# A cross-attention kernel: scores from two fp32r parts in 64-row tiles in place of three bf16 parts

## The chip, the cores and the metric

The kernel runs on one core of a Trainium2 chip. The metric is device time in microseconds of one execution, the median of several runs; lower is better.

## What is computed

Two cross-attention blocks follow each other on the same context, for four batch entries. The first has layer norms, 16 heads of 16 columns, and an MLP with GELU; the second has one head over 256 columns. Cut to what matters here:

```python
# first block: x is 4 x 256 x 256, context 4 x 512 x 256
q = (layer_norm(x) @ q_w + q_b)          # 16 heads of 16
k = (ctx @ k_w + k_b)
v = (ctx @ v_w + v_b)
scores = einsum('bhqd,bhkd->bhqk', q, k) * 16 ** -0.5
attn = softmax(where(mask, scores, lowest), axis=-1)
h = (attn @ v) @ cproj_w + cproj_b + x
h = h + gelu(layer_norm(h) @ fc_w + fc_b) @ proj_w + proj_b
# second block, one head: softmax(h wq (ctx wk).T / 16) (ctx wv) wo
return h + alpha * delta
```

## The kernel before

The five engines have a program each, written out by hand, and meet at semaphores. The unit of order is a slot. A batch entry has NG = 4 groups of GH = 4 heads, a group has SLOTS = 8 slots, so 32 slots a batch entry; slot s of a group is head s // 2. Each engine walks the slots in `iteration` (three levels by batch entry: the entry's attention, the projections of the next one, `pre`, and the rest of both blocks of the one before, `post`). Tables say in which slot a step stands: PRE_AT and EARLY_AT for `pre`, POST_AT and LATE_AT for `post`, PREP_AT for weights, TAIL_AT for the last entry.

**Precision by parts.** Products of projections and MLP are made of two fp32r parts of each operand (high, and the rest) and three matmuls (`product` L585, `products` L593; lines L589, L602, L606). The scores are made otherwise: queries and keys are split in three bf16 parts each, and the six products of TERMS_Q and TERMS_K are stacked along the contraction: `q_stack` and `k_stack` hold per head 6 x 16 rows of parts, one row for the mask (ones against `mask_row`), and 12 rows for the row maxima (three bf16 parts of each of four heads' maxima in `q_stack`, selectors in `k_stack`), 109 rows in all. So one bf16 matmul gives the whole score.

**A group's way.** `max_tile` (TensorE, L652) computes scores with the queries stationary and 512 keys moving, 97 rows; VectorE's `take_max` (L1442) takes the negated maximum over the keys, from one of three banks of `s1`. After the eight tiles of a group POOL's `split_max` (L1763 to L1769, four short operations) splits the maxima into three parts in `max_cols`. `max_rows` (TensorE, L659) transposes them in two matmuls, ScalarE's `rows` (L1100) copies them into `q_stack`. Then `exp_tile` (TensorE, L669) computes the scores again the other way round, keys stationary and 256 queries moving, two matmuls a slot, with the maximum already taken off; ScalarE's `exp` (L1109) writes `probs`, and `pv` (TensorE, L679) multiplies by `vals` with the denominator's column of ones, four heads in four column tiles of 17 columns. The maxima of group g+1 are made in the slots in which the exponent tiles of group g are made (MAX_TILES: two tiles in slots 0 and 1, one in slots 2 to 5; the split in slot 5, the transposes in slot 6). In a slot TensorE's order is: max tiles, `pre`, `post` or weight step, exp tile, in slots 1 and 3 the value product, in slot 6 the transposes of the maxima.

**Queries and keys.** For the queries (`pre`, U_Q) ScalarE writes the value `qf` (L1070) and its high part (L1072), then frees the bank; POOL takes the rest (L1785), ScalarE the middle part (L1087), POOL the low part (L1789). For each half of the keys VectorE writes `kf` (L1421), ScalarE the high part (L1092), POOL the rest (L1793), ScalarE the middle part (L1096), POOL the low part (L1797). In the prologue VectorE does POOL's operations for the first.

**Stack transfers.** SP moves the parts into the stacks by DMA, 16 partitions and four heads at a time: per group six transfers of queries (`stack_queries`, L518), six of keys (L529) and one of the mask row (L523), 13 in all, after the group's exponent tiles of the batch entry before are done. In the prologue ScalarE's queue (L1083) and POOL's (L1876) issue some of them. The selector rows are written once (L1320, L1322).

The file's other names on which a step rests: `ft[2]`, the third scratch of the GELU, lies over `qf`, so POOL's third square waits for `q_parts`.

## Time and profile before

| | us |
|---|---|
| median of 3 runs | 314.64 |
| lowest and highest | 312.69, 316.79 |
| span of the profiled execution | 310.4 |
| TensorE (PE) busy in it | 268.6 |
| VectorE (DVE) busy | 206.8 |
| ScalarE (ACT) busy | 187.8 |
| POOL busy | 118.3 |

The profile is of one execution of its own, and its span runs from the first to the last instruction; the page gives no other time for it. Busy time of PE is the union of its matmuls' records, which overlap: a matmul's start is recorded, its end is modelled. So how fast TensorE goes is read from the distance of starts, and a busy PE may still stand between two matmuls. An x4 in a row of the timeline merges four instructions of one line; plain fp32 matmuls leave two records each. The moving type of fp32r matmuls reads f32 (those of L589, L602 and L606 are fp32r). A wait is put down to whoever came last.

### The profile page before, as it was taken

To read this page: it belongs to the slowest core of one execution; us is meant where nothing else is said; L and a number is where in the kernel's file an instruction comes from. 1 tells how busy PE (TensorE), PEld (TensorE's weight loads), DVE (VectorE), ACT (ScalarE), POOL (GpSimd) and SP (SyncE) were. 2 spreads that over 40 slices of the span, in tenths; PEclk is the share of its full clock that TensorE was granted. 3 is DMA by queue.
4 is the path that set the end of the run, shared out by engine and by line. 5 is a ranking of instruction groups with operands and counts; after the bars stand their busy time and mean duration, and the time that the engine had idled before them with its cause. 6 is when DMAs were issued, how large, how long until landed. Compare 5 with 4: busy or idle time off the path is not lost.

```text
span 310.4 us, 5591 instructions
## 1 busy us (share of the span) xinstructions
PE 268.6 (87%) x2073; PEld 195.3 (63%) x2073; DVE 206.8 (67%) x367; ACT 187.8 (61%) x351; POOL 118.3 (38%) x174
## 2 busy tenths in 40 slices
PE   3974769998788999899979997999998989898995
PEld 2670236683266676665866766665966777677974
DVE  5774777729657859576569598657388655366854
ACT  1553367759464686967454887766466678426622
POOL 3574652523111369830012688430131256324100
PEclk9997599989797999999999999999999999999999
DMA  5597552522254002124112112121130000000001
GB/s 176 173 155 104 141 157 94 163 72 67 78 154 126 12 25 67 57 74 126 64 38 99 28 59 70 34 80 51 34 130 3 0 1 2 2 0 0 2 34 36
DMA packets 21163, 21.62 MB, mean 70 GB/s; under 512 B 4608, under 2 KB 17616, under 8 KB 21136
## 3 DMA queue, kind: packets, MB, share of 16 engines
q1 hardware_dynamic: 16880, 13.09, 14.8%
q0 software_dynamic: 1648, 3.87, 4.9%
q10 hardware_dynamic: 2608, 4.30, 4.6%
q8 instruction: 17, 0.28, 0.4%
q14 instruction: 10, 0.08, 0.1%
HBM read 10.50 MB, written 1.05 MB: 37 GB/s over the span
## 4 chain that ended last, share of the span: by engine, by line
PE 56%; ACT 13%; POOL 11%; DVE 9%; issue 5%; DMA 3%; ACTq 2%; POOLq 0%; DVEq 0%
PE work_ps L602 10%; PE om L679 8%; PE s L652 7%; PE work_ps L589 6%; PE s L669 6%; PE work_ps L606 5%; DVE neg_max L1442 4%; ACT q_stack L1100 3%; ACT probs L1109 2%; POOL y_l L1833 2%; PE s L602 2%; DMA q_stack<-qp 2%; POOL kf L1793 1%; ACT fx L1136 1%; POOL ft L1828 1%
## 5 line engine op out<-in xcount | busy, mean ns | idle before, releaser
L1442 DVE TENSOR_REDUCE neg_max<-s 128x1 f32<-128x512 f32 x128 | 83.5, 683 | 23.1 <-PE s L652 21.9
L1109 ACT ACTIVATE probs<-s 128x512 f32<-128x512 f32 x128 | 75.3, 601 | 32.4 <-PE s L669 31.8
L652 PE MATMUL s<-k_stack,q_stack 97*128 97x512 bf16 x128 | 49.8, 424 | 8.2 <-DMA q_stack<-qp 4.9
L669 PE MATMUL s<-q_stack,k_stack 109*128 109x256 bf16 x256 | 51.8, 286 | 2.0 <-ACT probs L1109 1.0
L679 PE MATMUL om<-probs,vals 128*17 128x256 f32 x512 | 34.5, 390 | 0.2 <-ACT probs L1109 0.2
L669 PEld LDWEIGHTS s<-q_stack,k_stack 109*128 109x128 bf16 x256 | 21.0, 102 | 19.0 <-ACT probs L1109 5.0
L652 PEld LDWEIGHTS s<-k_stack,q_stack 97*128 97x128 bf16 x128 | 13.0, 102 | 28.8 <-DVE neg_max L1442 14.3
L1763 POOL CAST max_cols<-neg_max 128x8 bf16<-128x8 f32 x16 | 6.1, 381 | 63.2 <-DVE neg_max L1442 63.2
L1100 ACT ACTIVATE q_stack<-om 13x1024 bf16<-13x1024 bf16 x16 | 16.3, 1017 | 9.1 <-PE om L659 8.8
L679 PEld LDWEIGHTS om<-probs,vals 128*17 128x17 f32 x512 | 12.0, 98 | 13.7 <-issue 6.2
L1123 ACT ACTIVATE y_h<-work_ps 128x512 fp32r<-128x512 f32 x12 | 7.2, 596 | 16.3 <-PE work_ps L606 14.5
L1453 DVE TENSOR_TENSOR y_l<-work_ps,y_h 128x512 fp32r<-128x512 f32 x12 | 8.3, 688 | 12.0 <-ACT y_h L1123 12.0
L1510 DVE SCALAR_TENSOR_TENSOR ft<-ft,fx 128x512 f32<-128x512 f32 x9 | 10.0, 1109 | 6.6 <-POOL ft L1828 6.6
L1833 POOL TENSOR_TENSOR y_l<-fx,y_h 128x512 fp32r<-128x512 f32 x9 | 13.3, 1484 | 2.5 <-ACT y_h L1162 2.5
L602 PE MATMUL work_ps<-wp_h,y_h 128*128 128x256 f32 x48 | 13.2, 310 | 0.5 <-DVE kf L1421 0.5
L1828 POOL TENSOR_TENSOR ft<-fx 128x512 f32<-128x512 f32 x9 | 9.4, 1042 | 11.0 <-ACT fx L1136 11.0
L659 PE MATMUL om<-ident_b,max_cols 128*109 128x128 bf16 x32 | 4.9, 236 | 9.9 <-POOL max_cols L1769 9.9
L1754 POOL TENSOR_TENSOR ln<-ln,minus_half 128x2 f32<-128x2 f32 x8 | 6.0, 754 | 18.5 <-DVE ln L1390 18.3
L1793 POOL TENSOR_TENSOR kf<-kf,kp 128x512 f32<-128x512 f32 x7 | 8.2, 1164 | 12.5 <-ACT kp L1092 12.5
L602 PE MATMUL work_ps<-aT_h,wf_h 128*128 128x256 f32 x48 | 12.8, 300 | 0.0
L1843 POOL TENSOR_TENSOR pc_l<-pcx,pc_h 128x1024 fp32r<-128x1024 f32 x3 | 7.1, 2373 | 12.7 <-ACT pc_h L1174 12.7
L602 PE MATMUL work_ps<-aT_h,wf_l 128*128 128x256 f32 x48 | 11.8, 280 | 0.0
(328 smaller groups left out, 724.5 us busy)
## 6 DMA issues: line engine op xcount, KB each, us to landing
k_stack<-kp SPq DMA_DIRECT2D x96, 64.0 KB
q_stack<-qp SPq DMA_DIRECT2D x81, 32.0 KB
cx<-in_ctx_dram SPq DMA_DIRECT2D x4, 512.0 KB, 4.7
pcx<-in_ctx_dram ACTq DMA_DIRECT2D x3, 512.0 KB, 3.6
xz<-in_x_dram SPq DMA_DIRECT2D x4, 256.0 KB, 2.7
raw_late<-in_L_xattn_fc_w_dram POOLq DMA_DIRECT2D x1, 1024.0 KB, 5.4
raw_late<-in_L_xattn_proj_w_dram POOLq DMA_DIRECT2D x1, 1024.0 KB, 6.7
h<-in_x_dram ACTq DMA_DIRECT2D x3, 256.0 KB, 2.6
```

The lines of the kernel that those rows point to most:

```text
L589: mm = pe.matmul(o, wi(w[a], k), vi(v[c], k), start=start and k == 0 and i == 0, stop=stop and k == n - 1 and i == 2)
L602: pe.matmul(o, wi(w[a], k), vi(v[c], k), start=start and i == k == a == c == 0, stop=False)
L606: mm = pe.matmul(o, wi(w[late[0]], k), vi(v[late[1]], k), start=False, stop=stop and i == len(terms) - 1 and k == n - 1)
L652: pe.matmul(s1[:, s1_bank(b, SLOTS * g + s), :], q_stack[0:ROW_MAX, hd, chunk(t)], k_stack[0:ROW_MAX, hd, :], start=True, stop=True).then_ ...
L669: mm = pe.matmul(s2[:, s2_bank(b, SLOTS * g + s), i * LQ:(i + 1) * LQ], k_stack[:, hd, chunk(k)], q_stack[:, hd, :], start=True, stop=True)
L679: mm = pe.matmul(om[32 * j:32 * j + VW, 0:LQ], vals[:, k, j * NG + g, :], probs[:, g % 2, j, k, :], start=k == 0, stop=k == TK - 1)
L1100: act.activation(q_stack[ROW_MASK:ROWS, g * GH:(g + 1) * GH, :], om_rows[ROW_MASK:ROWS, :].unsqueeze(1).to_broadcast([ROWS - ROW_MASK, GH, ...
L1109: act.activation(probs[:, g % 2, s // 2, k:k + 2, :], s2[:, s2_bank(b, SLOTS * g + s), :].rearrange("p (k n) -> p k n", k=2), ACT.Exp).the ...
L1442: dve.tensor_reduce(neg_max[:, g % 2, s % 2, s // 2:s // 2 + 1], s1[:, s1_bank(b, SLOTS * g + s), :], AX.X, ALU.max, negate=True).then_inc ...
L1793: pool.tensor_tensor(kf[:], kf[:], kp[:, 0, c, :], ALU.subtract).then_inc(kr_done, 1)
L1828: pool.tensor_tensor(ft[i % 3], fx[i % 3], fx[i % 3], ALU.mult).then_inc(square, 1)
L1833: pool.tensor_tensor(lo, fx[i % 3], hi.bitcast(F32), ALU.subtract).then_inc(y_split, 1)
```

## The change

Queries and keys are split in two fp32r parts, and the scores are three products (high high, high low, low high), as in the rest of the kernel. A stack has 57 rows: eight for the maxima (two parts of four heads), one for the mask, 48 for the products, in fp32r, and groups 0 and 2 lie in partitions 0 to 63, groups 1 and 3 in 64 to 127. So the score matmuls of a group use one half of the array's rows, and maxima and exponent tiles that stand beside each other use different halves. The max tile takes all 57 rows, with zeros in the rows of the maxima, which a transfer of its own, `stack_first`, puts back before each group; a group has eight transfers (three of queries, three of keys, one of the mask row, one of first rows). For the queries ScalarE writes the high part (two activations) and VectorE the low part from the bank; for each half of the keys VectorE writes the value, ScalarE the high part, POOL the low part. `split_max` has two operations. The transposes of the maxima are fp32, of 72 columns. In the prologue the selector rows are written by VectorE and copied by three transfers of SP, which also puts the first rows of all four groups, before it loads the second context.

```diff
-HC = P // HD
 SLOTS = 8
 VW = HD + 1
-TERMS_Q = (0, 0, 1, 0, 1, 2)
-TERMS_K = (0, 1, 0, 2, 1, 0)
-ROW_MASK = len(TERMS_Q) * HD
-ROW_MAX = ROW_MASK + 1
-ROWS = ROW_MAX + 3 * GH
+TERMS_Q = (0, 0, 1)
+TERMS_K = (0, 1, 0)
+HALF = P // 2
+ROW_MASK = 2 * GH
+ROW_TERM = ROW_MASK + 1
+ROWS = ROW_TERM + len(TERMS_Q) * HD
+MAX_COLS = HALF + ROW_MASK
...
-STACK_DMAS = 2 * len(TERMS_Q) + 1
+STACK_DMAS = 2 * len(TERMS_Q) + 2
...
-        with nc.sbuf_tensor("q_stack", [ROWS, H, LQ], BF16) as q_stack, nc.sbuf_tensor("k_stack", [ROWS, H, LK], BF16) as k_stack:
+        kp = pair("kp", [P, DC, LK])
+        with nc.sbuf_tensor("q_stack", [P, H // 2, LQ], F32R) as q_stack, nc.sbuf_tensor("k_stack", [P, H // 2, LK], F32R) as k_stack:
...
+        first_rows = rows[P // 4:P // 4 + ROW_TERM, 0:LQ]
...
+        def slots_of(g):
+            return slice(g // 2 * GH, (g // 2 + 1) * GH)
+        def stack_rows(g, first, n):
+            return slice(g % 2 * HALF + first, g % 2 * HALF + first + n)
+        def words(ap):
+            return ap.bitcast(F32)
+        def term_rows(g, i):
+            return stack_rows(g, ROW_TERM + i * HD, HD)
...
             def stack_queries(b, g):
-                made = ((pre_free, pre_use(b, U_Q)), (qm_done, b + 1), (q_parts, b + 1))
-                for part, (sem_, n) in enumerate(made):
-                    sp.wait_ge(sem_, n)
+                for part, (made, n) in enumerate(((qh_done, b + 1), (pre_free, pre_use(b, U_Q)))):
+                    sp.wait_ge(made, n)
                     for i in [i for i, p in enumerate(TERMS_Q) if p == part]:
-                        sp.dma_start(q_stack[i * HD:(i + 1) * HD, group(g), :], qp[rows_of(g), part, g // 2, :]).then_inc(stacked[g], 16)
+                        sp.dma_start(words(q_stack[term_rows(g, i), slots_of(g), :]), words(qp[part][rows_of(g), g // 2, :])).then_inc(stacked[g], 16)
             def stack_keys(b, g):
                 c = g // 2
                 sp.wait_ge(row_done, b + 1)
-                sp.dma_start(k_stack[ROW_MASK:ROW_MASK + 1, group(g), :],
-                             mask_row[0:1, :].unsqueeze(1).to_broadcast([1, GH, LK])).then_inc(stacked[g], 16)
-                made = ((kh_done, 2 * b + c + 1), (km_done, 2 * b + c + 1), (k_parts, 2 * b + c + 1))
-                for part, (sem_, n) in enumerate(made):
-                    sp.wait_ge(sem_, n)
+                sp.dma_start(words(k_stack[stack_rows(g, ROW_MASK, 1), slots_of(g), :]),
+                             words(mask_row).unsqueeze(1).to_broadcast([1, GH, LK])).then_inc(stacked[g], 16)
+                for part, made in enumerate((kh_done, k_parts)):
+                    sp.wait_ge(made, 2 * b + c + 1)
                     for i in [i for i, p in enumerate(TERMS_K) if p == part]:
-                        sp.dma_start(k_stack[i * HD:(i + 1) * HD, group(g), :], kp[rows_of(g), part, c, :]).then_inc(stacked[g], 16)
+                        sp.dma_start(words(k_stack[term_rows(g, i), slots_of(g), :]), words(kp[part][rows_of(g), c, :])).then_inc(stacked[g], 16)
+            def stack_first(g):
+                sp.dma_start(words(q_stack[stack_rows(g, 0, ROW_TERM), slots_of(g), :]),
+                             words(first_rows).unsqueeze(1).to_broadcast([ROW_TERM, GH, LQ])).then_inc(stacked[g], 16)
             def stack_group(b, g):
                 await_(sp, s2_full, NS * (b - 1) + SLOTS * (g + 1))
+                stack_first(g)
                 stack_queries(b, g)
                 stack_keys(b, g)
...
+                sp.wait_ge(dve_const, 4)
+                for g in range(NG):
+                    stack_first(g)
+                for g in range(1, NG):
+                    sp.dma_start(words(k_stack[stack_rows(g, 0, ROW_MASK), slots_of(g), :]),
+                                 words(k_stack[stack_rows(0, 0, ROW_MASK), slots_of(0), :])).then_inc(sel_in, 16)
...
-                hd, t = g * GH + s // 2, s % 2
+                hd, t = g // 2 * GH + s // 2, s % 2
                 if s == 0:
                     await_stacked(pe, [g], b + 1)
+                    if b == 0:
+                        if g == 0:
+                            pe.wait_ge(dve_const, 4)
+                        else:
+                            pe.wait_ge(sel_in, 16 * (NG - 1))
...
-                pe.matmul(s1[:, s1_bank(b, SLOTS * g + s), :], q_stack[0:ROW_MAX, hd, chunk(t)], k_stack[0:ROW_MAX, hd, :],
+                half = stack_rows(g, 0, ROWS)
+                pe.matmul(s1[:, s1_bank(b, SLOTS * g + s), :], q_stack[half, hd, chunk(t)], k_stack[half, hd, :],
                           start=True, stop=True).then_inc(s1_full, 1)
...
-                hd = g * GH + s // 2
-                n = NS * b + SLOTS * g + s
+                hd = g // 2 * GH + s // 2
+                half = stack_rows(g, 0, ROWS)
                 await_(pe, s2_free, s2_before(b, SLOTS * g + s))
                 for i in range(2):
                     k = 2 * (s % 2) + i
-                    mm = pe.matmul(s2[:, s2_bank(b, SLOTS * g + s), i * LQ:(i + 1) * LQ], k_stack[:, hd, chunk(k)], q_stack[:, hd, :],
+                    mm = pe.matmul(s2[:, s2_bank(b, SLOTS * g + s), i * LQ:(i + 1) * LQ], k_stack[half, hd, chunk(k)], q_stack[half, hd, :],
...
                     await_stacked(act, range(NG), b)
-                    await_(act, q_parts, b)
-                    if b == 0:
-                        act.wait_ge(pre_free, pre_use(b, U_K))
                     for c in range(DC):
-                        act.activation(qf[:, c, :], pre_bank(b, n)[:, c * LQ:(c + 1) * LQ], ACT.Identity, bias=bq[:, c:c + 1])
-                    for c in range(DC):
-                        a = act.activation(qp[:, 0, c, :], pre_bank(b, n)[:, c * LQ:(c + 1) * LQ], ACT.Identity, bias=bq[:, c:c + 1])
-                    a.then_inc(pre_free, 1)
+                        a = act.activation(qp[0][:, c, :], pre_bank(b, n)[:, c * LQ:(c + 1) * LQ], ACT.Identity, bias=bq[:, c:c + 1])
+                    a.then_inc(qh_done, 1)
...
             def key_high(b, c):
-                await_stacked(act, (2 * c, 2 * c + 1), b)
                 act.wait_ge(pre_free, pre_use(b, U_K + c))
-                act.activation(kp[:, 0, c, :], kf[:], ACT.Copy).then_inc(kh_done, 1)
-            def key_middle(b, c):
-                act.wait_ge(kr_done, 2 * b + c + 1)
-                act.activation(kp[:, 1, c, :], kf[:], ACT.Copy).then_inc(km_done, 1)
-            def rows(b, g):
+                act.activation(kp[0][:, c, :], kp[1][:, c, :].bitcast(F32), ACT.Copy).then_inc(kh_done, 1)
+            def max_rows(b, g):
                 act.wait_ge(rows_ps, NG * b + g + 1)
-                act.activation(q_stack[ROW_MASK:ROWS, g * GH:(g + 1) * GH, :],
-                               om_rows[ROW_MASK:ROWS, :].unsqueeze(1).to_broadcast([ROWS - ROW_MASK, GH, LQ]),
+                of = stack_rows(g, 0, ROW_MASK)
+                act.activation(q_stack[of, slots_of(g), :], om_rows[of, :].unsqueeze(1).to_broadcast([ROW_MASK, GH, LQ]),
                                ACT.Copy).then_inc(rows_in, 1)
...
+                    await_stacked(dve, (2 * c, 2 * c + 1), b)
+                    dve.scalar_tensor_tensor(kp[1][:, c, :].bitcast(F32), pre_bank(b, n), bk[:, c:c + 1], mask_f[:], ALU.add, ALU.mult)\
                        .then_inc(pre_free, 1)
-            def query_rest(b):
-                dve.wait_ge(pre_free, pre_use(b, U_Q))
-                dve.tensor_tensor(qf[:], qf[:], qp[:, 0, :, :], ALU.subtract).then_inc(qr_done, 1)
-            def query_low(b):
-                dve.wait_ge(qm_done, b + 1)
-                dve.tensor_tensor(qp[:, 2, :, :], qf[:], qp[:, 1, :, :], ALU.subtract).then_inc(q_parts, 1)
-            def key_rest(b, c):
+                elif n == U_Q:
+                    dve.wait_ge(qh_done, b + 1)
+                    for c in range(DC):
+                        i = dve.scalar_tensor_tensor(qp[1][:, c, :], pre_bank(b, n)[:, c * LQ:(c + 1) * LQ], bq[:, c:c + 1],
+                                                     qp[0][:, c, :].bitcast(F32), ALU.add, ALU.subtract)
+                    i.then_inc(pre_free, 1)
+            def key_low(b, c):
                 dve.wait_ge(kh_done, 2 * b + c + 1)
-                dve.tensor_tensor(kf[:], kf[:], kp[:, 0, c, :], ALU.subtract).then_inc(kr_done, 1)
-            def key_low(b, c):
-                dve.wait_ge(km_done, 2 * b + c + 1)
-                dve.tensor_tensor(kp[:, 2, c, :], kf[:], kp[:, 1, c, :], ALU.subtract).then_inc(k_parts, 1)
+                dve.tensor_tensor(kp[1][:, c, :], kp[1][:, c, :].bitcast(F32), kp[0][:, c, :].bitcast(F32), ALU.subtract)\
+                   .then_inc(k_parts, 1)
...
-                key_rest(0, 0)
+                key_low(0, 0)
                 low_weights(wv[1][:], raw_v, wv[0][:], 2)
-                key_low(0, 0)
-                query_rest(0)
+                pre(0, U_Q)
                 dve.memset(om[:], 0.0).then_inc(post_free[0], 1)
-                query_low(0)
-                dve.memset(q_stack[ROW_MASK:ROWS, HC:H, :], 1.0).then_inc(dve_const, 1)
                 pre(0, U_K + 1)
                 dve.memset(vals[:, :, :, HD:VW], 1.0).then_inc(post_free[1], 1)
...
-                step = 3 * (NG * b + g)
-                part = [max_cols[:, :, ROW_MAX + i:ROWS:3] for i in range(3)]
+                part = [max_cols[:, :, g % 2 * HALF + i:g % 2 * HALF + ROW_MASK:2] for i in range(2)]
                 neg = neg_max[:, g % 2, :, :]
                 pool.wait_ge(s1_free, NS * b + SLOTS * (g + 1))
                 await_(pool, rows_ps, NG * b + g)
                 pool.tensor_copy(part[0], neg).then_inc(max_step, 1)
-                pool.wait_ge(max_step, step + 1)
-                pool.tensor_tensor(max_rest[:], neg, part[0], ALU.subtract).then_inc(max_step, 1)
-                pool.wait_ge(max_step, step + 2)
-                pool.tensor_copy(part[1], max_rest[:]).then_inc(max_step, 1)
-                pool.wait_ge(max_step, step + 3)
-                pool.tensor_tensor(part[2], max_rest[:], part[1], ALU.subtract).then_inc(max_split, 1)
+                pool.wait_ge(max_step, NG * b + g + 1)
+                pool.tensor_tensor(part[1], neg, part[0].bitcast(F32), ALU.subtract).then_inc(max_split, 1)
```

TensorE's order of instructions is unchanged. It matters which matmuls stand beside each other. The first piece is TensorE in the kernel before, at the end of group 0 and in group 1 of batch entry 0 (L669 exponent tiles, L652 max tiles, L679 value product, L659 transposes of the maxima, the others work on 128 rows):

```order
L652 MATMUL s<-k_stack,q_stack 128x512 x2
L625 MATMUL work_ps<-ident,cx 128x128 x4
L669 MATMUL s<-q_stack,k_stack 128x256 x2
L652 MATMUL s<-k_stack,q_stack 128x512 x2
L669 MATMUL s<-q_stack,k_stack 128x256 x2
L679 MATMUL om<-probs,vals 17x256 x8
L652 MATMUL s<-k_stack,q_stack 128x512
L620 MATMUL work_ps<-ident,xz 128x128 x4
L669 MATMUL s<-q_stack,k_stack 128x256 x2
L652 MATMUL s<-k_stack,q_stack 128x512
```

and the same place in the changed kernel (L693 exponent tiles, L676 max tiles, L703 value product):

```order
L676 MATMUL s<-k_stack,q_stack 128x512 x2
L643 MATMUL work_ps<-ident,cx 128x128 x4
L693 MATMUL s<-q_stack,k_stack 128x256 x2
L676 MATMUL s<-k_stack,q_stack 128x512 x2
L693 MATMUL s<-q_stack,k_stack 128x256 x2
L703 MATMUL om<-probs,vals 17x256 x8
L676 MATMUL s<-k_stack,q_stack 128x512
L638 MATMUL work_ps<-ident,xz 128x128 x4
L693 MATMUL s<-q_stack,k_stack 128x256 x2
L676 MATMUL s<-k_stack,q_stack 128x512
```

The rows are the same; L693 and L676 now use 57 rows in one half each, the others are as they were, so between L643, L638 or L703 and the score matmuls the shape of the tile changes, and between L693 and L676 the half.

The second piece is POOL in the middle of batch entry 1 (`qf` and `kf` the values of queries and keys, `ft`, `y_l` and `h` steps of the MLP, `max_cols` the split maxima), before:

```order
L1789 TENSOR_TENSOR qp<-qf,qp 128x512
L1828 TENSOR_TENSOR ft<-fx 128x512 x2
L1793 TENSOR_TENSOR kf<-kf,kp 128x512
L1797 TENSOR_TENSOR kp<-kf,kp 128x512
L1828 TENSOR_TENSOR qf<-z 128x512
L1833 TENSOR_TENSOR y_l<-fx,y_h 128x512 x2
L1828 TENSOR_TENSOR ft<-fx 128x512
L1820 TENSOR_TENSOR h<-h,pb 128x512
L1793 TENSOR_TENSOR kf<-kf,kp 128x512
L1763 CAST max_cols<-neg_max 128x2x4
L1765 TENSOR_TENSOR max_rest<-neg_max,max_cols 128x8
L1767 CAST max_cols<-max_rest 128x2x4
```

and in the changed kernel:

```order
L1794 TENSOR_TENSOR ft<-fx 128x512 x2
L1768 TENSOR_TENSOR kp_l<-kp_l,kp_h 128x512
L1794 TENSOR_TENSOR ft_third<-z 128x512
L1799 TENSOR_TENSOR y_l<-fx,y_h 128x512 x2
L1794 TENSOR_TENSOR ft<-fx 128x512
L1786 TENSOR_TENSOR h<-h,pb 128x512
L1768 TENSOR_TENSOR kp_l<-kp_l,kp_h 128x512
L1750 CAST max_cols<-neg_max 128x2x4
L1752 TENSOR_TENSOR max_cols<-neg_max,max_cols 128x2x4
```

The query's low part, one of the two operations of a key half (one subtraction stays, as `kp_l`) and two of the four of the split are gone.

The third piece is SP's queue in the prologue, from the biases on, before:

```order
L542 DMA bk<-in_L_xattn_k_b_dram 128x1x1 x2
L542 DMA qb<-in_L_xattn_q_b_dram 128x1x1 x2
L545 DMA cx<-in_ctx_dram 128x1024
L547 DMA raw_late<-in_L_xattn_w_q_dram 128x512
L547 DMA raw_late<-in_L_xattn_w_k_dram 128x512
L523 DMA k_stack<-mask_row 1x4x512
L529 DMA k_stack<-kp 16x4x512 x6
L551 DMA q_stack<-qp 16x4x256 x3
```

and in the changed kernel:

```order
L554 DMA bk<-in_L_xattn_k_b_dram 128x1x1 x2
L554 DMA qb<-in_L_xattn_q_b_dram 128x1x1 x2
L539 DMA q_stack<-rows 9x4x256 x4
L560 DMA k_stack<-k_stack 8x2048 x3
L563 DMA cx<-in_ctx_dram 128x1024
L565 DMA raw_late<-in_L_xattn_w_q_dram 128x512
L565 DMA raw_late<-in_L_xattn_w_k_dram 128x512
L530 DMA k_stack<-rows 1x4x512
L535 DMA k_stack<-kp_h 16x4x512 x2
L535 DMA k_stack<-kp_l 16x4x512
L569 DMA q_stack<-qp_h 16x4x256 x2
```

Seven transfers now stand ahead of the load of the second context, and the stacks of group 0 take six transfers of SP (mask row, three of keys, two of queries) where they took ten.

## Rows read from the trace of the kernel before

**Rows 1.** Page, part 1: busy us (share of the span) and instructions.

```profile
PE 268.6 (87%) x2073; PEld 195.3 (63%) x2073; DVE 206.8 (67%) x367; ACT 187.8 (61%) x351; POOL 118.3 (38%) x174
```

**Rows 2.** Waits of TensorE: us in total, times, longest.

```profile
PE om L659 <- POOL max_cols L1769: 9.9, 7, 2.0
...
PE s L652 <- DMA q_stack<-qp: 4.9, 1, 4.9
```

**Rows 3.** Three stretches: length, busy us (instructions) of each engine, clock, DMA share, GB/s.

```profile
18.00:27.00 9.00, 4.10 (x30) 3.52 (x28) 4.41 (x6) 4.02 (x5) 7.43 (x14) 0.97 1.09 166
27.00:35.00 8.00, 5.27 (x12) 1.03 (x10) 5.91 (x10) 1.81 (x4) 2.97 (x7) 0.50 0.33 63
...
90.00:155.00 65.00, 59.50 (x485) 44.41 (x484) 45.16 (x75) 43.30 (x83) 28.00 (x36) 0.97 0.22 69
```

**Rows 4.** Timeline of TensorE's matmuls near 170 and 230 us: start, us.

```profile
169.60 0.38 PE L652 MATMUL s<-k_stack,q_stack 97*128 97x512 bf16 x1
169.82 0.38 PE L669 MATMUL s<-q_stack,k_stack 109*128 109x256 bf16 x2
...
229.29 0.40 PE L589 MATMUL s<-cT_h,wv_l 128*128 128x512 f32 x1
229.52 0.40 PE L669 MATMUL s<-q_stack,k_stack 109*128 109x256 bf16 x2
229.85 1.06 PE L679 MATMUL om<-probs,vals 128*17 128x256 f32 x16
230.84 0.39 PE L652 MATMUL s<-k_stack,q_stack 97*128 97x512 bf16 x1
231.07 0.38 PE L669 MATMUL s<-q_stack,k_stack 109*128 109x256 bf16 x2
231.29 0.38 PE L652 MATMUL s<-k_stack,q_stack 97*128 97x512 bf16 x1
...
231.62 0.28 PE L602 MATMUL work_ps<-wc_l,aT_h 128*128 128x256 f32 x1
...
231.86 0.29 PE L602 MATMUL work_ps<-wc_l,aT_h 128*128 128x256 f32 x1
```

**Rows 5.** Chain of waits, one piece: start, us, what (eight plain fp32 records).

```profile
57.91 1.73 PE work_ps L956 x8
```

**Rows 6.** Page, part 5: VectorE's maxima; busy, mean ns, idle before.

```profile
L1442 DVE TENSOR_REDUCE neg_max<-s 128x1 f32<-128x512 f32 x128 | 83.5, 683 | 23.1 <-PE s L652 21.9
```

**Rows 7.** Timeline of TensorE around the four one-row matmuls, L982.

```profile
13.12 0.40 PE L589 MATMUL s<-cT_h,wk_l 128*128 128x512 f32 x1
13.45 0.60 PE L982 MATMUL s<-ident,oT 1*128 1x1 f32 x4
13.98 0.39 PE L589 MATMUL work_ps<-zT_h,wq_h 128*128 128x256 f32 x1
```

**Rows 8.** Timeline of POOL before the transposes at 128.3 us.

```profile
125.61 1.18 POOL L1793 TENSOR_TENSOR kf<-kf,kp 128x512 f32<-128x512 f32 x1 [0.65 <-ACT kp L1092]
...
127.48 0.21 POOL L1765 TENSOR_TENSOR max_rest<-neg_max,max_cols 128x8 f32<-128x8 f32 x1
127.75 0.21 POOL L1767 CAST max_cols<-max_rest 128x8 bf16<-128x8 f32 x1
```

**Rows 9.** Group of the query activations on ScalarE: busy, mean ns, idle before.

```profile
L1070 ACT ACTIVATE qf<-work_ps,bq 128x256 f32<-128x256 f32 x8 | 3.3, 468 | 4.8 <-PE work_ps L589 4.8
```

**Rows 10.** Chain of waits before the first score matmul: start, us, what.

```profile
16.33 0.82 ACT qf L1070 x2
17.15 0.74 ACT qp L1072 x2
...
18.63 0.64 ACT qp L1087
...
20.69 5.74 DMA q_stack<-qp
```

**Rows 11.** Timeline of SP: six transfers of key parts.

```profile
15.05 3.86 SPq L529 DMA_DIRECT2D k_stack<-kp  x6
```

More of the change, by code:

```diff
@@ L177, in build @@
         cx = sb("cx", [P, TK, D])
+        with nc.sbuf_tensor("ft_third", [P, 2 * LQ], F32) as ft_third:
+            pass
         zT = pair("zT", [P, DC, LQ])
@@ L1328, in prologue @@
                 pre(0, U_V + 1)
-                rows(0, 0)
+                max_rows(0, 0)
                 for s in range(START):
```

124 lines of the change are left out of this document (40 added, 84 removed).

## The prediction

> **What bounds the kernel now.** I read the page's engine shares first: TensorE is busy 268.6 of 310.4 us [rows 1], so it waits for 42 us in all. The list of its waits says for whom [rows 2]: 9.9 us in 7 waits for the last of POOL's operations that split the row maxima, and 4.9 us once for the first stack transfers; the others are small. The table by stretch [rows 3] shows where: from 90 to 155 TensorE is busy 59.50 of 65 us; only near the start does it idle, busy 4.10 of 9 us from 18 to 27 and 5.27 of 8 from 27 to 35, there at a granted clock of 0.50, the lower of its two levels (1.2 GHz). So outside the start the kernel runs at TensorE's pace. What the change does to TensorE's stream counts nearly in full, and work taken from other engines counts only where TensorE waits for it.
>
> **TensorE: the price of a score matmul.** In the timeline [rows 4] the next matmul starts 0.22 us after a bf16 one with 512 moving columns (169.60 to 169.82), and two bf16 ones with 256 take 0.22 (231.07 to 231.29). The fp32r matmuls that are there already take 0.23 for 512 columns (229.29 to 229.52) and 0.12 for 256 (231.62 to 231.86, two of them). The count of matmuls stays (128 of 512 columns, 256 of 256): six products of 16 rows were one matmul of 97 or 109 rows, three are one of 57. So the wider type costs 128 x 0.01 + 256 x 0.01, some 3.5 us. The 32 transposes of the maxima go from bf16 to fp32; that can't be more than the 0.12 of a 256-column fp32r matmul each, 3.8 us, and as they are half as wide and have a price already, I take 0.5. Together **+4 us**, bounds 0 and 7.
>
> **TensorE: the change of tile shape.** The scores now use 57 rows in one half of the array, while all other work takes the 128 rows. The trace has two cases of another shape. The value product (17 columns) takes tiles side by side: two scores before it take 0.33 us (229.52 to 229.85) where they take 0.22 before another score, so entering costs 0.11. Its 16 records take 0.99 (229.85 to 230.84); four at once make four packs, and at the 0.216 of a plain fp32 record (1.73 for 8, [rows 5]) these are 0.87, so leaving costs 0.12. And four matmuls of one row stand between full ones [rows 7]: the full one before them lasts 0.33 (13.12 to 13.45) and not 0.23; the four, 0.11 apart as narrow ones are, would end at 13.89, and the next full one starts at 13.98. So a change costs 0.09 to 0.12; I take 0.09, by the one-row case, which is the nearer. In the order of the changed kernel 98 runs of scores stand between other things, and neighbours of another shape meet 221 times where they met 62 times (in and out of the value product): 159 x 0.09 = 14.3 us. Where TensorE waits for another engine at that place, the change hides; by the idle 42 us of 310 and as much again inside its busy time that is one place in five: **+11.5 us**. Bounds: 0, if two halves are no other shape than the whole, and 159 x 0.12 = 19.
>
> The Trainium skill (TensorEngine Tiling (Array Packing), Key Properties) says that changing the tiling mode, not only the tile, drains TensorE. Here the drain is not whole: the record of the two scores ends at 229.92 and the value product starts at 229.85 [rows 4]. A whole drain would add those 0.07 to each change.
>
> **TensorE: two halves at once.** The maxima of group g+1 lie in the other half than the exponent tiles of group g, and go to another bank. No row shows two row halves at work. But the value product's 16 records of 0.216 take 0.99 and not 3.5 us, so tiles side by side do run together. I count a run's gain from the order: in "exp exp max max" (14 runs) the second exp hides under the first max, 0.11; "max exp exp max" (11) and "max exp exp max exp exp" (7) save 0.22, "exp exp max" (6) 0.11; 41 runs "exp exp" and 13 of a lone max save nothing; longer ones up to 1.3. The sum is 12.7 us; the lower bound is 0. It is lost where the next max waits for a bank that VectorE still reduces (683 ns each [rows 6], against 440 of a slot's scores), above all in the long runs near 35 us. I take three quarters, **-9 us**.
>
> The Trainium skill (TensorE: Matmul & The Clock Gate, Packing small matmuls) measured 3.07 times for four row tiles; by that the gain would be three quarters too. No run here shows it yet.
>
> **POOL and ScalarE.** Before each pair of transposes POOL does four operations; the short ones take 0.21 and start 0.27 apart [rows 8]. Two go: 0.56 us, in 7 waits 3.9. In two of them (at 128 us, and a batch later) the splits come late because POOL is still at "kf", 1.18 [rows 8]; in the changed order one of the two operations per key half is gone, so a further 0.8 falls away in each. **-5.5 us**; bounds -3.9 and -9.9. ScalarE loses two query activations of 0.47 [rows 9] a batch, which must be done before the queries' bank is free, and three middle parts. That is on TensorE's way in the first batch at most: **-0.7**, bounds 0 and -3.8. VectorE gains two operations of 256 columns a batch, some 0.35 each by the 683 ns of its 512 columns [rows 6]; TensorE's other bank covers it, uncovered it is +2.1 for three batches.
>
> **The start.** The chain there [rows 10]: two query activations (0.82), two more (0.74), a rest on VectorE, a middle part on ScalarE (0.64), the issues, then 5.74 us until the last has landed; TensorE idles 4.9 [rows 2]. Now it is two activations, two short operations on VectorE, and one issue, and ScalarE has no key middle part ahead of them. The last issue comes some 3 us sooner. Against that, the transfer engines are full from 18 to 27 (share 1.09 [rows 3]) and the bytes are the same; and SP issues seven more transfers at the beginning, 7 x 0.64 = 4.5 us by its 3.86 for six [rows 11], most of it in time that it idles. I take **-3 us**, bounds 0 and -4.9. In the steady part 8 issues a group instead of 13 free 3.2 us of SP, but no wait of TensorE names a transfer there: nothing.
>
> **Sum.** 310.4 + 4 + 11.5 - 9 - 5.5 - 0.7 - 3 = 307.7 us. The profiled execution shows no time but its span, 310.4; the median of the runs, 314.6, is 4.2 above it. 307.7 + 4.2 = 311.9: **312 us**, 0.8% less than before. About 2% (6.3 us) is what a measurement of this kernel can tell from no change.
>
> **Rivals.**
> 1. The halves switch for free. For: the array is not regrouped by columns, as it is in the row that shows most of the price. Against: the one-row matmuls pay as well. Then the 11.5 go: 300.5 us, faster.
> 2. Slower: the changes of shape eat everything. If each drains the array wholly, it costs 0.09 + 0.07 = 0.16, and 159 x 0.16 = 25.4 in place of 11.5: 326 us. If it is the overlap that fails, because rows of 4 bytes in both halves can't be fed at once, 312 + 9 = 321. It is over 2% slower from 0.15 a change on. For: 41 runs are two small matmuls alone between two changes. Against: [rows 4, 7]. The Trainium skill's rule above, taken at its word, gives this 326.
> 3. The first transfers land no sooner, since the transfer engines are full: 315 us, the rest as forecast.
> 4. POOL sets the pace before 128 us and a batch later, and more than the two waits goes, up to 3 us at each: 306 us. Against: TensorE is busy 59.5 of 65 us there [rows 3].
>
> **Chances.** Forecast 0.40, rival 3 0.12, rival 1 0.18, rival 4 0.13, rival 2 0.17. Faster is rival 1 and rival 4, 0.31. Within 2% is the forecast with rival 3, less 0.04 for the forecast's own upper tail: 0.48. Slower is rival 2 and that tail, 0.21. The range leaves out the lower half of rival 1 and the full drain: 302 to 322.
>
> **What would show it.** Right: a max and an exp of the other half start well under 0.1 us apart; two exps followed by a full matmul take 0.32 us and not 0.23; the waits for the splits fall from 9.9 to under 5 us; the first max starts near 23.5 us. Wrong: exps followed by full matmuls still at 0.23 (rival 1) or at 0.4 (rival 2); max and exp 0.22 apart everywhere; the first max still near 26.5 (rival 3).

## The result, and the profile after

The changed kernel takes 327.75 us (median of 4 runs, 327.16 to 328.75), the kernel before, run beside it, 314.41 (4 runs, 312.69 to 316.79): a ratio of 1.043 with a 95% interval of 1.037 to 1.048. It is slower by 4%, where 312 us and a range up to 322 were forecast. Here and below a time is the median of all runs of a kernel, while a ratio and its interval leave out runs over 1.5% above the kernel's fastest, so that it is not always the ratio of the medians. The spans are 310.4 and 325.3 us, the mean granted clocks 0.960 and 0.941.

The page's line of engine shares, which answers to [rows 1]:

```profile
PE 293.2 (90%) x2073; PEld 212.3 (65%) x2073; DVE 204.3 (63%) x372; ACT 176.2 (54%) x330; POOL 92.8 (29%) x122
```

The work of every other engine went down; TensorE, with the same 2073 matmuls, is busy for 25 us more. Its waits, which answer to [rows 2]:

```profile
PE s L676 <- issue: 4.4, 1, 4.4
PE om L683 <- POOL max_cols L1752: 4.1, 5, 1.7
```

The wait for the splits fell from 9.9 to 4.1 us, as forecast. The wait of 4.9 us before the first max matmul is still there as 4.4: no gain at the start. The stretches of [rows 3], and the one behind them:

```profile
18.00:27.00 9.00, 4.62 (x32) 4.28 (x31) 0.82 (x3) 2.41 (x4) 3.31 (x5) 0.84 1.03 168
27.00:35.00 8.00, 5.86 (x11) 2.30 (x11) 5.76 (x9) 0.25 (x1) 1.33 (x4) 0.50 0.97 132
35.00:50.00 15.00, 14.69 (x72) 9.27 (x75) 11.35 (x23) 9.15 (x16) 6.59 (x12) 0.57 0.46 144
90.00:155.00 65.00, 61.20 (x440) 43.34 (x442) 43.77 (x77) 39.99 (x77) 21.77 (x24) 0.95 0.23 62
```

From 90 to 155 us TensorE gets 440 matmuls done where it did 485. Two things are to be read in its timeline (start, us). First a lone pair of exp matmuls. Of the 109 runs of score matmuls 41 are such pairs, 24 between full-array work and 17 ahead of a value product. Before:

```profile
255.80 0.51 PE L606 MATMUL work_ps<-aT_l,wf_h 128*128 128x256 f32 x3
256.15 0.39 PE L669 MATMUL s<-q_stack,k_stack 109*128 109x256 bf16 x2
256.38 0.49 PE L843 MATMUL s<-ident,oT 128*128 128x128 f32 x3
```

and the same place after, with two places where both halves are at work:

```profile
121.29 0.50 PE L676 MATMUL s<-k_stack,q_stack 57*128 57x512 f32 x1
121.30 0.50 PE L693 MATMUL s<-q_stack,k_stack 57*128 57x256 f32 x2
...
128.44 0.38 PE L693 MATMUL s<-q_stack,k_stack 57*128 57x256 f32 x1
128.44 0.50 PE L676 MATMUL s<-k_stack,q_stack 57*128 57x512 f32 x1
128.66 0.28 PE L693 MATMUL s<-q_stack,k_stack 57*128 57x256 f32 x1
128.87 0.39 PE L620 MATMUL work_ps<-wp_h,y_h 128*128 128x256 f32 x1
129.10 0.28 PE L620 MATMUL work_ps<-wp_l,y_h 128*128 128x256 f32 x1
...
269.40 0.51 PE L624 MATMUL work_ps<-aT_l,wf_h 128*128 128x256 f32 x3
269.84 0.50 PE L693 MATMUL s<-q_stack,k_stack 57*128 57x256 f32 x2
270.27 0.55 PE L867 MATMUL s<-ident,oT 128*128 128x128 f32 x3
```

The pair takes 0.43 us up to the next work (269.84 to 270.27) where it took 0.23, and it starts 0.21 behind the matmul before it, not 0.12: 0.29 us more for a pair, in the median of the pairs between full-array work too, where two changes of shape at 0.09 had been counted. And there is more behind it. The first full fp32r product behind a run of scores holds the next one off by 0.23 (128.87 to 129.10), where 256 columns take 0.12 in a row; the first transpose behind a run 0.16 and not 0.11. Seven pairs stand between fp32r products. From the matmul ahead of such a pair to the third product behind it, the median went from 0.59 to 0.99 us. The overlap is real: at 121.29 a max and an exp matmul start together.

Last, the clock. It fell to 0.50 at 24 us and was back at 48; before, it had fallen at 26 and was back at 40. One minus the mean clock, times the span, is called the lost clock here: 12.4 us before, 19.2 after. It is not all lost time, as TensorE also waits in such stretches.

### The profile page after: what moved, and what is told of

Read it like the earlier page. It is cut to its first block, busy times and chain, and to the rows that moved or that the text cites. A ratio compares the mean times of both kernels' runs of the same rounds, so it can differ in the third digit from the quotient of the medians.

```text
span 325.3 us, 5437 instructions
## 1 busy us (share of the span) xinstructions
PE 293.2 (90%) x2073; PEld 212.3 (65%) x2073; DVE 204.3 (63%) x372; ACT 176.2 (54%) x330; POOL 92.8 (29%) x122
## 4 chain that ended last, share of the span: by engine, by line
PE 72%; DVE 8%; ACT 7%; issue 4%; POOL 4%; SPq 4%; DMA 1%; POOLq 0%; ACTq 0%; DVEq 0%
PE work_ps L620 13%; PE s L693 9%; PE om L703 9%; PE s L676 8%; PE work_ps L607 8%; PE work_ps L624 6%; DVE neg_max L1431 4%; PE s L607 2%; PE s L620 2%; PE om L683 2%; ACT probs L1118 2%; PE work_ps L753 1%; DMA raw_late<-in_L_xattn_w_k_dram 1%; ACT q_stack L1110 1%; PE work_ps L972 1%
## 5 line engine op out<-in xcount | busy, mean ns | idle before, releaser
L676 PE MATMUL s<-k_stack,q_stack 57*128 57x512 f32 x128 | 56.2, 505 | 7.2 <-issue 4.4
L693 PE MATMUL s<-q_stack,k_stack 57*128 57x256 f32 x256 | 61.2, 342 | 1.6 <-ACT probs L1118 1.4
L693 PEld LDWEIGHTS s<-q_stack,k_stack 57*128 57x128 f32 x256 | 38.8, 200 | 19.4 <-issue 8.4
L676 PEld LDWEIGHTS s<-k_stack,q_stack 57*128 57x128 f32 x128 | 23.8, 208 | 26.3 <-issue 13.4
L703 PE MATMUL om<-probs,vals 128*17 128x256 f32 x512 | 35.3, 397 | 0.1
L1750 POOL CAST max_cols<-neg_max 128x8 fp32r<-128x8 f32 x16 | 5.9, 368 | 89.1 <-DVE neg_max L1431 89.1
L1110 ACT ACTIVATE q_stack<-om 8x1024 fp32r<-8x1024 f32 x16 | 16.1, 1009 | 13.5 <-PE om L683 13.3
L703 PEld LDWEIGHTS om<-probs,vals 128*17 128x17 f32 x512 | 12.2, 99 | 11.7 <-issue 1.5
L1799 POOL TENSOR_TENSOR y_l<-fx,y_h 128x512 fp32r<-128x512 f32 x9 | 12.4, 1384 | 5.3 <-ACT y_h L1171 5.3
L1768 POOL TENSOR_TENSOR kp_l<-kp_l,kp_h 128x512 fp32r<-128x512 f32 x7 | 9.0, 1281 | 16.7 <-ACT kp_h L1105 16.7
L1145 ACT ACTIVATE fx<-work_ps,bf 128x256 f32<-128x256 f32 x18 | 7.6, 471 | 9.9 <-PE work_ps L624 9.9
L620 PE MATMUL work_ps<-wp_l,y_h 128*128 128x256 f32 x48 | 11.9, 280 | 0.0
```

The lines of the kernel that those rows point to most:

```text
L620: pe.matmul(o, wi(w[a], k), vi(v[c], k), start=start and i == k == a == c == 0, stop=False)
L676: pe.matmul(s1[:, s1_bank(b, SLOTS * g + s), :], q_stack[half, hd, chunk(t)], k_stack[half, hd, :], start=True, stop=True).then_inc(s1_ful ...
L693: mm = pe.matmul(s2[:, s2_bank(b, SLOTS * g + s), i * LQ:(i + 1) * LQ], k_stack[half, hd, chunk(k)], q_stack[half, hd, :], start=True, sto ...
L703: mm = pe.matmul(om[32 * j:32 * j + VW, 0:LQ], vals[:, k, j * NG + g, :], probs[:, g % 2, j, k, :], start=k == 0, stop=k == TK - 1)
L1110: act.activation(q_stack[of, slots_of(g), :], om_rows[of, :].unsqueeze(1).to_broadcast([ROW_MASK, GH, LQ]), ACT.Copy).then_inc(rows_in, 1)
L1799: pool.tensor_tensor(lo, fx[i % 3], hi.bitcast(F32), ALU.subtract).then_inc(y_split, 1)
```

## The experiments

All ratios are to the kernel before, run on the same chip in between; one hundredth is 3.1 us. Eight of the kernels keep every transfer, wait and instruction of the changed kernel and alter only the operands of its score matmuls (with one copy on ScalarE added), so that shape, type and rows can be set apart.

**e0_ctl**, the control.

```
+ still = sb("still", [P, P], F32R)
...
- pe.matmul(s1[...], q_stack[half, hd, chunk(t)], k_stack[half, hd, :],
+ pe.matmul(s1[...], still[half, :], still[half, :].unsqueeze(1).to_broadcast([HALF, 4, P]),
...
- mm = pe.matmul(s2[...], k_stack[half, hd, chunk(k)], q_stack[half, hd, :],
+ mm = pe.matmul(s2[...], still[half, :], still[half, :].unsqueeze(1).to_broadcast([HALF, 2, P]),
...
+ act.activation(still[:], raw_v[:, 0, 0:P], ACT.Copy)
```

> The control for the next three. The changed kernel, whose score matmuls read a constant fp32r tensor of 128 columns (repeated along the moving side) in place of the two stacks, in the same halves of the rows and in the same order; every transfer, wait and other instruction stays, and one copy on ScalarE in the prologue is added. It leaves out the true scores. All theories: as the changed kernel, 327 to 329 us. If it comes out elsewhere, the repeated operand has a price, and the next three are read against this run.

Measured: 327.9 us, 1.039 (1.027 to 1.051). The lone pair takes 0.430. The stand-in is good.

**e1_full**: the same with `still[:, :]`, all 128 rows.

> As the control, but both operands of a score matmul span all 128 rows: fp32r stays, the 64-row tiles go, and with them 159 changes of shape and all overlap of the halves. It leaves out the true scores. Theory A (a change of shape costs 0.2 us, the half that the prediction saw and as much again behind the recorded start): 159 changes give back 32 us, the lost overlap takes some 10: 306 us, and a lone pair of exp matmuls takes 0.23 to 0.24 us up to the next full one, not 0.43. Theory B (a change costs 0.16, as rival 2 had it): 312. Theory C (the loss is the start and its transfers, or fp32r itself): 320 to 328.

Measured: 314.6 us, 1.002 (0.997 to 1.006). The pair takes 0.241 and starts 0.118 behind. With all 128 rows the loss is gone, so it lies in the tiles, or in the fewer rows that they use (e16_f77, below, sets these apart); the start and its transfers, still as in the changed kernel, are none of it. But 306 was missed: fp32r has a price of its own (below, e8_bffull).

**e2_low**: the same with `still[0:HALF, :]`.

> As the control, but every score matmul reads rows 0 to 63: the tiles and their changes stay, and no two score matmuls lie in different halves, so none can overlap. It leaves out the true scores. Theory A, with the overlap worth about what the prediction gave it (9 us): 336 to 340 us, with the run max exp exp max some 0.4 us longer. If the overlap had failed in the changed kernel: no change, 328.

Measured: 345.9 us, 1.091 (1.079 to 1.103), above the forecast. "max exp exp max" behind a value product takes 0.892, where the control takes 0.661: 0.23 longer, not the 0.4 expected. So the overlap is worth 16 us (0.052), more than the 9 forecast and the 10 expected here. Between the two profiled runs the difference is 14.0 us, and e2_low loses 6.8 us more clock (25.6 as against 18.8), so a part of the 16 may be clock.

**e3_bf16**: the control with `still` in bf16.

> As the control, but the constant tensor is bf16: 64-row tiles in alternate halves as before, with bf16 weights. It leaves out the true scores. Theory A (half of the price of a change is the load of 128 fp32r columns that nothing hides, at the entry to the score matmuls): 98 runs of scores save 0.1 us each at their entry, and the changes inside a run as much: 314 to 318 us. Theory D (a change costs 0.2 us whatever the type of the weights, because the array drains): 326 to 328.

Measured: 316.7 us, 1.010 (1.007 to 1.014), as theory A had it. The pair takes 0.320 and starts 0.211 behind: the entry still costs 0.09, the 0.11 behind the recorded start is gone. The first full fp32r product behind a run still holds the next one off by 0.22.

**e8_bffull**: bf16 and all 128 rows.

> As e1_full (both operands of a score matmul are a constant over all 128 rows), but bf16 in place of fp32r. It leaves out the true scores. What is left of the change is then the fewer transfers and the shorter splits alone. Theory A (the full-shape fp32r run gave back at its matmuls what the splits gained: behind a value product its max matmul took 0.340 us, not 0.226): bf16 saves 28 such entries by 0.11 and some 0.01 to 0.02 on the other 300 matmuls, 5 to 8 us: 307 to 310 us, which makes the splits and transfers worth 5 to 7. Rival: the shorter splits were worth nothing on this path: 313 to 315.

Measured: 308.15 us, 0.979 (0.971 to 0.988), as theory A had it. What is left of the change without tiles and fp32r is a gain of 6.6 us (with 128 rows, where the kernel before uses 97 and 109); fp32r at full shape costs 7.1 (0.0225). The timelines behind a value product show where: a lone max ahead of transposes took 0.340 up to the next matmul with fp32r, as against 0.226 with bf16.

**e14_bflow**: e8_bffull with `still[0:HALF, :]`.

> As e8_bffull (bf16, constant operands, 308 us), but every score matmul reads rows 0 to 63, so that 159 neighbours differ in shape and nothing overlaps. It leaves out the true scores. Theory A (a change costs 0.09 with bf16 weights, the half that the prediction saw, and fp32r weights add 0.11 where they are loaded first): 159 x 0.09 = 14 us more: 321 to 324. Theory D (about 0.2 a change for any type, as e2_low against e1_full gives for fp32r, 31 us): 335 to 340.

Measured: 337.7 us, 1.068 (1.062 to 1.073), as theory D had it, 24 us above the same matmuls over 77 rows (e15_rows77, below). A pair in its timeline:

```profile
282.78 0.52 PE L625 MATMUL work_ps<-aT_l,wf_h 128*128 128x256 f32 x3
283.23 0.39 PE L694 MATMUL s<-still 64*128 64x256 bf16 x2
283.55 0.55 PE L868 MATMUL s<-ident,oT 128*128 128x128 f32 x3
```

This takes 0.32, and 0.21 to start: 0.09 a change, as theory A had it up to the recorded starts. But the first full fp32r product behind a run holds the next off by 0.22 here too, so a pair between such products costs 0.28 us more than in e15_rows77 (0.88 as against 0.59, measured as above), not 0.18. What the changes are worth in time is seen where the clock is full. From the 61st of the 109 runs of scores to the end e14_bflow takes 142.2 us (from 195.9) and e15_rows77 136.7 (from 173.8), with 75 of the 159 changes: 0.07 each, 12 us in all. By this estimate the other 12 of the 24 come with the clock, which neither theory had: its mean is 0.90 and 0.91 in the two shortest runs, as against 0.94 to 0.96 in e15_rows77. In the profiled run, one of the two longer ones, it is 0.884, and the clock is at 0.50 from 26 to 60 us and from 73 to 104.

**e5_start**: the changed kernel, six of its seven first transfers moved.

```
  sp.wait_ge(dve_const, 4)
- for g in range(NG): stack_first(g)
- for g in range(1, NG): sp.dma_start(words(k_stack[...]), ...)
+ stack_first(0)
  ...
  stack_keys(0, 1)
  stack_queries(0, 1)
+ for g in range(1, NG): stack_first(g)
+ for g in range(1, NG): sp.dma_start(words(k_stack[...]), ...)
```

> The changed kernel, whose seven new transfers at the start are moved: one (group 0's constant rows) stays ahead of the second batch's load of cx, the other six go behind group 1's first transfers. Expected: the load of cx and the two loads behind it are issued some 3 us earlier (before 10.1 us), TensorE's wait for its weights (WA) goes, and the first max matmul starts at 24 to 25.5 us, not 26.6. Theory A (the start is a small part of the loss): 325 to 327 us. Theory C (the start with its full DMA queues and low clock from 23 to 45 us is the loss): under 320. Rival: the first max waits for a transfer that the full DMA engines land no sooner: no change, 328.

Measured: 329.8 us, 1.052 (1.045 to 1.058). SP issued the load of cx at 7.5 us, not 10.1, and the first max started at 26.50, not 26.58. So the load was issued earlier and the first max gained nothing, as the rival had it: the first score matmul does not hang on SP's queue. TensorE waits 5.2 us before it, and 1.7 before the first max of the second group (36.3 us), which needs the moved transfers; the changed kernel has no such second wait. The ratio is 0.009 above that of the changed kernel, with an interval of 0.008.

**e4_order** and **e6_border**: one move in the order of TensorE, in the kernel after and in the kernel before.

```
  for at, ab, g, s, attends in slots(b, last):
-     if attends:
-         attend(ab, g, s, 0)
      ...
      if attends:
+         attend(ab, g, s, 0)
          attend(ab, g, s, 1)
```

> The changed kernel with one thing moved on TensorE: in each slot the max matmuls of the group ahead are issued right before the exp matmuls, behind the slot's other work, not before it. Counted in the program: 96 runs of score matmuls, not 109; 208 changes of shape, not 221; and nearly every max matmul gets exp matmuls of the other half beside it (by 0.32 us for a max and 0.215 for an exp on each half, 30.6 us are overlapped, not 21.9). Theory A (0.2 us for a change, overlap in full): 13 x 0.2 + 8.6 = 11 us less: 315 to 319. Rival (a max that comes later stretches the waits of DVE and of the maxima, and takes it all back): 325 to 330.

> The same move in the kernel before the change, as the control for e4_order: full-array bf16 score matmuls, where neither shape nor overlap can gain. Theory A: no gain, 313 to 317 us. If the order itself (when the maxima come) is worth something, it shows here too.

Measured: 339.2 us, 1.081 (1.075 to 1.087), and 329.4 us, 1.052 (1.044 to 1.060). Both expectations fell. The later maxima cost the kernel before 16 us: its waits for the splits rose by 2.5 us to 12.4, and its clock, back at 40 us, fell again from 44 to 51 (20.5 us of clock lost, as against 12.4). In the changed kernel the same move costs 12, so fewer changes and more overlap gave back 4 us, not 11, and with an interval of 4 to either side even these are hardly told from nothing. An order made for overlap pays only where nothing waits for what moves back.

**e12_split**: the kernel before with a split in two.

```
- pool.tensor_tensor(max_rest[:], neg, part[0], ALU.subtract).then_inc(max_step, 1)
- pool.wait_ge(max_step, step + 2)
- pool.tensor_copy(part[1], max_rest[:]).then_inc(max_step, 1)
- pool.wait_ge(max_step, step + 3)
- pool.tensor_tensor(part[2], max_rest[:], part[1], ALU.subtract).then_inc(max_split, 1)
+ pool.tensor_tensor(part[1], neg, part[0], ALU.subtract).then_inc(max_split, 1)
```

> The kernel before with one part of the change alone: POOL splits the negated maxima into two parts with two instructions, not three with four (the third column stays zero, so a third part of each maximum is left out). If the split's two instructions are what the shape-free version e8_bffull gained (6 us in all), TensorE's wait for them falls from 9.9 us to about 6 and the time by 3.5 to 5: 309 to 311 us. Rival (the gain was in the transfers): 313 to 315.

Measured: 308.5 us, 0.987 (0.981 to 0.992): the shortest time here of a kernel with true scores. The gain is under the 2% that one measurement can tell, but its interval is clear of 1. TensorE's wait for the splits:

```profile
PE om L659 <- POOL max_cols L1764: 6.1, 7, 1.4
```

3.8 us less than in [rows 2], and the time is 4.2 less by the ratio. This is the part of the change that was worth making.

**e9_two** and **e13_both**: four products of two bf16 parts; the second with e12_split's edit as well.

```
- TERMS_Q = (0, 0, 1, 0, 1, 2)
- TERMS_K = (0, 1, 0, 2, 1, 0)
+ TERMS_Q = (0, 0, 1, 1)
+ TERMS_K = (0, 1, 0, 1)
```

> The kernel before with four products in place of six: the terms with third parts go and middle by middle is added, which keeps the contraction above 64 rows (65 for the maxima, 77 for the exp matmuls), so the full array; 9 transfers per group, not 13. The third parts are still made, and used nowhere. Fewer transfers alone: the DMA share falls, TensorE waits for no transfer but the first. Expected 311 to 315 us: within what a measurement can tell; if the transfers were what e8_bffull gained, 308 to 310.

> e12_split and e9_two in one: full array, bf16, two parts of q, k and the maxima, four products, 9 transfers. Nothing of the 64-row tiles and nothing of fp32r. Theory A (the useful half of the change is the short split and the fewer transfers, and it needs the full array): as e8_bffull, 306 to 310 us, which would beat both kernels. Rival (no part of it counts): 313 to 315.

Measured: 320.9 us, 1.014 (1.009 to 1.019), and 318.2 us, 1.012 (1.006 to 1.018). Both theories fell: less work everywhere, no change of shape, matmuls as fast as before (a pair 0.231), and no gain but a loss of 1.2 to 1.4%, under 2% but with intervals clear of 1. TensorE's wait for the first transfers fell from 4.9 to 1.4 us, yet more was lost with the clock: back at 50 us, not at 40, with a mean of 0.935 and 0.940 in the profiled runs (20.5 and 18.9 us of clock lost, as against 12.4) and down to 0.91 in the others. Apart from the transfers these two have one thing in common with the 64-row tiles: fewer rows of the array are used, 65 and 77 instead of 97 and 109.

**e15_rows77** and **e16_f77** change that alone: e8_bffull and e1_full with `still[0:77, :]`, which is still the shape of the full array.

> As e8_bffull (bf16, constant operands, one shape for all work), but a score matmul spans 77 of the 128 rows, which is still the full-array shape. It leaves out the true scores. The question is what holds the granted clock down after the first maxima: it is back at about 38 us in e8_bffull and e12_split, at 50 in e9_two and e13_both, whose score matmuls span 65 and 77 rows and whose first max starts some 3 us earlier. Theory R (fewer rows at work keep the clock low): it comes back at 46 us or later, mean clock 0.93 to 0.95, 314 to 320 us. Theory S (the earlier start does it, the rows do nothing): as e8_bffull, back at 38, mean clock 0.97, 306 to 310 us.

> The same with fp32r: e1_full (314.6 us, clock back at 38 us) with 77 of the 128 rows. It leaves out the true scores. Theory R: back at 46 us or later, 320 to 327 us. Theory S: 313 to 316 us.

Measured: 312.3 us, 0.990 (0.985 to 0.996), and 321.4 us, 1.021 (1.014 to 1.027). Theory R holds in its mechanism: against the same kernel with 128 rows it is +3.6 us (0.0113) with bf16, a time between the ranges of both theories, and intervals that still overlap a little, and +6.0 (0.019) with fp32r, clear of noise and inside the range of theory R. The mean clock tells them apart in every run: 0.966 to 0.977 with 128 rows and bf16, 0.935 to 0.956 with 77; 0.962 to 0.977 and 0.930 to 0.936 with fp32r. The chip is not the reason: the kernel before had 0.935 to 0.962 beside those with 128 rows and 0.934 to 0.956 beside those with 77. Three stretches with 128 rows (e8_bffull; the clock is the third number from the end):

```profile
35.00:40.00 5.00, 4.82 (x20) 2.09 (x20) 4.45 (x9) 3.41 (x7) 2.24 (x4) 0.70 0.49 145
40.00:45.00 5.00, 2.94 (x21) 1.96 (x21) 3.88 (x12) 3.42 (x7) 3.51 (x7) 1.00 0.27 74
45.00:50.00 5.00, 5.00 (x56) 3.05 (x56) 4.82 (x8) 3.35 (x8) 0.00 (x0) 1.00 0.49 196
```

and with 77 (e15_rows77):

```profile
35.00:40.00 5.00, 4.54 (x18) 2.07 (x17) 4.45 (x11) 3.47 (x6) 1.05 (x4) 0.50 0.58 139
40.00:45.00 5.00, 4.63 (x19) 2.83 (x18) 3.33 (x7) 3.19 (x5) 3.12 (x5) 0.50 0.52 156
45.00:50.00 5.00, 5.00 (x36) 2.27 (x37) 2.64 (x5) 1.77 (x4) 0.00 (x0) 0.56 0.31 114
```

From 35 to 40 us TensorE is about as busy in both. With 128 rows the clock is full again at 38 us, and TensorE then even waits; with 77 rows it is back at 49 us only, and from 45 to 50 TensorE gets 36 matmuls done, not 56. As the clock also fell later with 77 rows (29 us, not 24), it was low for 20.5 us in place of 13.7; with fp32r for 27.3 (26 to 53) in place of 6.8 (31 to 38). The lone pair takes the same 0.23 in both where the clock is full. Theory S, that an earlier start does it, is weaker but not wholly out: the first max of these two starts at 25.5 and 25.7 us, 1.0 and 1.3 earlier than with 128 rows. e2_low and the control, which both start at 25.8 to 26.0 and use 64-row tiles, are back at 50 and 47; the changed kernel, which starts at 26.6 like the kernel before, at 48, and e14_bflow, which starts at 26.5 like e8_bffull, at 60.

## Why the prediction was wrong, step by step

The ladder before, e8_bffull, e1_full, e16_f77, e2_low, e0_ctl goes through the parts of the change one at a time: -6.6 (splits, transfers, start, with 128 rows), +7.1 (fp32r), +6.0 (77 rows in place of 128), +22.1 (159 changes of shape), -16.3 (overlap), in all +12.3 us, with the changed kernel itself at +13.4. Each step has the clock that goes with it inside, and an interval of 3 to 6 us to either side.

- **The change of shape, forecast +11.5, measured +22.** This is the step that failed most. The rule was right (159 more neighbours, each with a price), the size was not: "a change costs 0.09 to 0.12; I take 0.09" was read up to the recorded start of the matmul entered. Where that one has fp32r weights, another 0.11 lies behind its start. On the way in, the first exp matmul of a pair holds the second off for 0.22 us, not 0.12, which e3_bf16 takes away. On the way out it stays whatever the type of the scores, as the products behind them are fp32r. So going in costs 0.20 and going out 0.19 before a product and 0.14 before transposes. As an estimate from these rows, 80 ways in, 39 out to products and 40 out to transposes cost 16 + 7.4 + 5.6 = 29 us. Where the clock is full, from the 61st run of scores to the end, e2_low takes 147.5 us (from 193.1) and e16_f77 138.6 (from 180.1), with 75 of the 159 changes: 0.12 each, 19 us in all. So about a third of the price is hidden; the forecast took one place in five, though its own 42 us of 310 and as much again are 27%. The trace of before had the part behind the start, one line behind [rows 7]:

```profile
14.20 0.29 PE L589 MATMUL work_ps<-zT_l,wq_h 128*128 128x256 f32 x1
```

From 13.98 the first full fp32r matmul behind the narrow ones holds the next off until 14.20, though it has 256 columns. The records of the exp matmuls' weight loads differ in the same sense: 102 ns in the mean before (bf16), 200 after (fp32r). The Trainium skill (TensorE: Matmul & The Clock Gate, Weight-path perf modes - Fast Weight Load (FWL) and DoubleRow) says that the fast load of 128 columns of weights is there for all types but fp32 (it does not name fp32r); that would fit the 0.11, and the trace agrees as far as bf16 does not show it. Rival 2 had named 326 us, by 0.16 a change, and its mark, a pair at 0.4, came true. Its mechanism, a whole drain of the array, was not it: with bf16 going in costs 0.09. Two slips on the way changed little: the scores stand in 109 runs, not 98 (the 221 and 62 neighbours are right), and by its own sum the kernel is over 2% slower from 0.13 a change on, not 0.15.
- **The clock, no term at all.** The forecast took the clock of before for given. About 7 us more of it are lost in the changed kernel (19.2 as against 12.4), 4 of them between 40 and 48 us. e15_rows77 and e16_f77 show that fewer rows do this, at 4 to 6 us. Of the 22 us for the shapes with fp32r some 19 are there at a full clock too, so about 3 are left for the clock; of the 24 with bf16 (e14_bflow) 12 are left for it. Why the clock loses so much more there is open.
- **The overlap, forecast -9, measured -16.** Right in its mechanism and in its mark (max and exp start 3 ns apart). "max exp exp max" saves 0.23 us (0.892 to 0.661), as counted, and "exp exp max" 0.23 (0.66 to 0.435), where 0.11 was counted; over six such runs that is not a microsecond. What makes up the rest of the difference is not shown; the 6.8 us of clock that e2_low loses beyond the control are the first candidate.
- **The type, forecast +4 (0.5 of it for the transposes, which lie in the step before), measured +7**, with an interval of 3: besides the 0.01 to 0.02 of each matmul it is the 0.11 again, at those that follow a value product.
- **POOL and ScalarE, forecast -6.2, and the start, forecast -3; both together measured -6.6.** The splits gave 4.2 by themselves, the wait under 5 us came true. The start gave nothing: the first max is at 26.58, before it was at 26.57. That is rival 3: the last stack transfer of group 0 was issued by 19.24 us, not 21.3, and the max still had to wait, with the transfer engines full (share 1.03 from 18 to 27, and now 0.97 from 27 to 35 as well, where it was 0.33).

That TensorE sets the pace was right, that its stream counts nearly in full less so, as a third of the price of the changes is hidden. All gains elsewhere (POOL 25 us less busy, ScalarE 12, a third fewer packets) were worth 6.6 us.

## What to carry to other kernels

On an engine that sets the pace, count how often a short run of small-tile matmuls is entered and left, and price both ends of it up to the second start, not the first. Here going in costs 0.20 us with fp32r weights and 0.09 with bf16, and going back to fp32r products 0.19 in either case, of which about a third was hidden. Overlapping halves give back 0.23 us in a run such as "exp exp max" and nothing in a lone pair, and 41 of these 109 runs were lone pairs. Before fewer rows are put through the array, look at where the granted clock is low: with the same count of matmuls and columns it stayed low for longer here, and took back what smaller transfers and shorter chains had gained.

## What was not expected of the hardware

- Matmuls of different halves start out of order. In the program the order at 128.44 us is exp, exp, max; the records show exp at 128.435, max at 128.442 and the second exp at 128.655, and six of the runs "exp exp max" read so. The max is hidden wholly: such a run takes 0.435 us, a pair alone 0.431. The Trainium skill (TensorE: Matmul & The Clock Gate, The mechanism) has matmuls start and end strictly in the order of the program; these recorded starts differ, and the measurement decides. The ends are modelled and show nothing on their order.
- The number of rows that a matmul spans, 77 or 128, left its duration alone and moved the granted clock: low for 20.5 and 13.7 us around the first maxima (bf16), for 27.3 and 6.8 (fp32r).
- The first matmul with fp32r weights behind a change of shape holds the next one off by 0.11 us, into the tiles and out of them; in a row of equal shape nothing of it shows.
